# Moving the last softmax, four ternary weight slices, the first FFN product and the last FFN outputs of a transformer block on one core

## The reference

```
x = x + xattn(layernorm(x), ctx_768)        # keys and values from 1601 context rows
x = x + attn(layernorm(x))                  # 16 heads, softmax over 64 keys
x = x + ffn(layernorm(x))

scores = einsum('bhid,bhjd->bhij', q, k) / sqrt(dh)
scores = clip(scores, -1e5, 1e5) + einsum('bhid,ijd->bhij', q, rel_pos)
attn = softmax(scores); attn = attn / (attn.sum(-1) + 1e-8)

scale = max(mean(|w|), 1e-8); w_t = clip(round(w / scale), -1, 1)   # ternary
out = gelu(x @ w_t1.T + b1) @ w_t2.T + b2                           # 2048 hidden units
```

## Time and profile before

| what | value |
|---|---|
| median of 3 runs | 558.68 us (558.35 to 562.51) |
| the profiled execution, own time | 557.74 us |
| its span | 556.0 us |
| busy share of the span: PE, DVE, ACT, POOL | 93%, 63%, 35%, 35% |
| mean granted PE clock | 0.991 of full |

### The profile page before, as it was taken

How to read it: one execution, slowest core, us unless ns; L and a number is a source line. 1 busy time by engine, 2 the same in 40 slices (tenths; PEclk the granted TensorE clock), 3 DMA queues, 4 the chain that set the end, 5 groups by cost and what they waited for, 6 DMA issues and landing times.

```text
span 556.0 us, 10383 instructions
## 1 busy us (share of the span) xinstructions
PE 517.0 (93%) x4137; PEld 295.8 (53%) x4137; DVE 349.0 (63%) x777; ACT 196.4 (35%) x455; POOL 193.7 (35%) x132
## 2 busy tenths in 40 slices
PE   4987789987999999999999999999988879999997
PEld 2634245653764855666485575666574334444443
DVE  5747484384768459377665845957596895435333
ACT  0333014424623541653373355145143552211110
POOL 0221234224306244440821524359364992000000
PEclk9997899999999999999999999999999999999999
DMA  8999599499499779859959986953527420002002
GB/s 294 418 381 418 194 361 374 148 367 302 178 386 254 282 285 269 325 208 367 264 208 382 256 309 242 230 195 146 115 77 190 152 75 1 0 1 77 0 2 75
DMA packets 42096, 122.45 MB, mean 220 GB/s; under 512 B 19640, under 2 KB 21432, under 8 KB 37312
## 3 DMA queue, kind: packets, MB, share of 16 engines
q1 hardware_dynamic: 24256, 109.20, 54.3%
q10 hardware_dynamic: 17792, 12.58, 9.6%
HBM read 111.29 MB, written 10.49 MB: 219 GB/s over the span
## 4 chain that ended last, share of the span: by engine, by line
PE 58%; DVE 14%; DMA 8%; issue 7%; POOL 5%; ACT 4%; SPq 3%; ACTq 0%; DVEq 0%; POOLq 0%
PE u_ps L927 12%; PE s_ps L1158 9%; PE w_ps L1143 8%; DMA area<-in_nat_dram 6%; PE u_ps L848 5%; PE s_ps L837 5%; PE w_ps L950 4%; DVE area L1253 3%; POOL area L418 2%; PE w_ps L859 2%; PE w_ps L941 2%; DMA area<-in_kt_dram 2%; PE w_ps L913 1%; DVE area L1343 1%; DVE area L1301 1%
## 5 line engine op out<-in xcount | busy, mean ns | idle before, releaser
L1253 DVE BATCH_NORM_STATS2 area<-area 128x6 f32<-128x384 f32 (+1 forms) x208 | 99.8, 546 | 30.1 <-DMA area<-in_nat_dram 30.1
L927 PE MATMUL u_ps<-area 128*64 128x384 f32 (+1 forms) x416 | 74.1, 500 | 5.0 <-DVE area L1319 5.0
L837 PE MATMUL s_ps<-area 128*64 128x512 f32 (+1 forms) x384 | 69.2, 503 | 2.4 <-DMA area<-in_kt_dram 1.3
L1158 PE MATMUL s_ps<-area 128*128 128x512 f16 x256 | 60.2, 378 | 4.8 <-DVE area L1557 4.8
L453 POOL TENSOR_SCALAR area<-area 128x512 f16<-128x512 f32 x32 | 55.8, 1760 | 15.3 <-DMA area<-in_wf_dram 15.3
L1143 PE MATMUL w_ps<-area 128*128 128x512 f16 x256 | 60.7, 378 | 0.2 <-ACT area L734 0.2
L418 POOL TENSOR_TENSOR area<-area 128x16 f32<-128x16 f32 (+1 forms) x16 | 39.1, 2441 | 48.0 <-DVE area L1268 48.0
L734 ACT ACTIVATE area<-w_ps,area 128x512 f32<-128x512 f32 x32 | 22.0, 688 | 79.4 <-PE w_ps L1143 74.0
L927 PEld LDWEIGHTS u_ps<-area 128*64 128x64 f32 (+1 forms) x416 | 27.9, 137 | 39.2 <-issue 30.8
L1301 DVE CUSTOM_DVE_ANT_0 area<-w_ps,area 128x512 f32<-128x512 f32 x24 | 15.4, 690 | 52.6 <-PE w_ps L810 52.6
L837 PEld LDWEIGHTS s_ps<-area 128*64 128x64 f32 x384 | 23.2, 136 | 40.0 <-issue 35.4
(11 more groups left out here) (177 smaller groups left out, 832.4 us busy)
## 6 DMA issues: line engine op xcount, KB each, us to landing
area<-in_kt_dram SPq DMA_DIRECT2D x24, 1536.0 KB, 8.4
area<-in_nat_dram SPq DMA_DIRECT2D x48, 768.0 KB, 9.6
area<-in_wf_dram SPq DMA_DIRECT2D x32, 256.0 KB, 8.8
skew<-area ACTq DMA_DIRECT2D x8, 1024.0 KB, 8.8
area<-in_wf_dram SPq DMA_DIRECT2D x16, 512.0 KB, 3.4
area<-in_aw_dram SPq DMA_DIRECT2D x4, 1024.0 KB, 12.9
area<-skew ACTq DMA_DIRECT2D x16, 256.0 KB, 12.9
area<-in_x_dram SPq DMA_DIRECT2D x8, 256.0 KB, 11.3
```

Of the source, the lines that this page charges most:

```text
L837: ins = pe.matmul(S[ch][u * L:(u + 1) * L, 0:n], a_sb[:, c, u * L:(u + 1) * L], x[:, u, c, :], start=(c == 0), stop=(c == KC - 1))
L927: ins = pe.matmul(U[u * L:(u + 1) * L, 0:DC], pT[g % 2][0:m, i, u * L:(u + 1) * L], nat[0:m, j, u, :], start=(j == 0), stop=(j == NJ - 1))
L1158: ins = pe.matmul(S[q], g[i % 3][:, q * P:(q + 1) * P], wf16[:, f, 1, :], start=(f == 0 and z == 0), stop=(f == KF - 1 and z == 1))
L1253: dve.bn_stats(st[b][0:m, 2 * j + u, :], nat[0:m, j, u, :]).then_inc(s["key_stats"], 1)
```

## The change

1. **Last softmax.** The operations of tile 7 stand apart, one behind the `parts` of a slice each: add at i = 1, maximum at 2, subtraction at 3, exponential on ACT at 5, `row_scale` behind `parts(5)`, product behind `parts(6)`. `PROBS_AT` goes from 6 to 8, `VALUES_AT` from 8 to 10, `O_AT` from 9 to 11, `Z7_AT` from 12 to 14, `Z6_AT` from 1 to 2.
2. **Ternary slices.** Slices 0 to 2 lie over the folded query-key weights, slice 3 over another row that is free by then, so `ternary(0)` to `ternary(3)` stand in step 7. Eleven slices stand before the loop instead of eight. POOL's comparisons move with them: `neg(5)` into step 7, `neg(6)` to `neg(10)` ahead of the reciprocal root of tile 6.
3. **First FFN product.** `hidden(0)` stands ahead of `att_o(6)` and `values(7)` on PE.
4. **Last outputs.** `last_out` does the two last output steps token tile by token tile: for each of the four tiles the matmuls of i = 30 and i = 31, then its semaphore.
5. In step 7 ACT does `cT_out` and `skew_load` ahead of `ctx_out`; in the bridge the softmax of tile 6 starts ahead of `v_out(6)`.

```diff
-        wf16, at = carve(NAT_AT, [P, KF, 2, CW], F16)
+        wf16, at = [], WQK_AT
+        for f in range(KF):
+            if f == 3:
+                assert at <= WQK_END
+                at = WROW_AT
+            elif f == 4:
+                at = NAT_AT
+            v, at = carve(at, [P, 2, CW], F16)
+            wf16.append(v)
-        AHEAD = HIGH_ON_ACT = 8
-        Z6_AT, PROBS_AT, VALUES_AT, O_AT, Z7_AT, EXP_AFTER = 1, 6, 8, 9, 12, 2
+        AHEAD, HIGH_ON_ACT = 11, 8
+        Z6_AT, EXP_AT, PROBS_AT, VALUES_AT, O_AT, Z7_AT = 2, 5, 8, 10, 11, 14
...
@@ gpsimd
                     neg(4)
+                    neg(5)
...
             row_rstd(LAST_T - 2, "ln2_var", "ln2_rstd", VE2, RS2)
-            neg(5)
+            neg(6)
             add_fb2(LAST_T - 2)
-            for f in range(6, 8):
+            for f in range(7, 11):
                 neg(f)
             row_rstd(LAST_T - 1, "ln2_var", "ln2_rstd", VE2, RS2)
             add_fb2(LAST_T - 1)
-            for f in range(8, KF):
+            for f in range(11, KF):
                 neg(f)
@@ scalar, step
                     probs_out(r)
+                if not more:
+                    cT_out(p)
+                    skew_load(t)
+                if r is not None:
                     ctx_out(r)
-                cT_out(p)
-                if t is not None:
+                if more:
+                    cT_out(p)
+                if t is not None and more:
                     skew_load(t)
@@ tensor
+            def last_out():
+
+                h = 1
+                for q in range(4):
+                    for i in (2 * KF - 2, 2 * KF - 1):
+                        if q == 0:
+                            pe.wait_ge(s["gelu_low"], i + 1)
+                        for z, g in enumerate((gh, gl)):
+                            ins = pe.matmul(S[q], g[i % 3][:, q * P:(q + 1) * P], wf16[i - h * KF][:, 1, :], start=False,
+                                            stop=(i == 2 * KF - 1 and z == 1))
+                    ins.then_inc(s["ffn_out_ps"], 1)
+
+            hidden(0)
+            att_o(LAST_T - 1)
+            values(LAST_T)
+            for i in range(1, 2 * KF):
...
-                if i < 2 * KF:
-                    hidden(i)
+                hidden(i)
                 if i >= 2:
                     ffn_out(i - 2)
+            last_out()
@@ vector, ternary
                 if f == 0:
+                    dve.wait_ge(s["a_ps"], NT)
+                if f == 3:
+                    dve.wait_ge(s["cq_terms"], NT)
+                if f == 4:
                     dve.wait_ge(s["tile_weighted"], NJ * NT)
@@ vector, step
                 pt_scale(p, 2)
+                if not more:
+                    ternary(0)
                 pt_scale(p, 3)
                 if not more:
+                    ternary(1)
+                    ternary(2)
                     return
@@ vector, bridge
-            v_out(LAST_T - 1)
-            row_shift(LAST_T - 1)
-            ternary(3)
+            row_add(LAST_T - 1)
+            row_max(LAST_T - 1)
+            row_shift(LAST_T - 1)
+            v_out(LAST_T - 1)
             row_scale(LAST_T - 1)
+            row_product(LAST_T - 1)
             z_low(LAST_T - 2)
-            ternary(4)
+            ternary(6)
             clip(LAST_T)
-            ternary(5)
+            ternary(7)
+            ternary(8)
             x2_sum(LAST_T - 1)
             x2_norm(LAST_T - 1)
-            ternary(6)
+            ternary(9)
             v_out(LAST_T)
-            ternary(7)
+            ternary(10)
@@ vector, loop
-                if i == EXP_AFTER:
-                    row_shift(LAST_T)
-                if i == EXP_AFTER + 1:
-                    row_scale(LAST_T)
-                if i == O_AT:
-                    x2_sum(LAST_T)
+                if i == O_AT + 1:
                     x2_norm(LAST_T)
                 parts(i)
+                if i == EXP_AT - 4:
+                    row_add(LAST_T)
+                if i == EXP_AT - 3:
+                    row_max(LAST_T)
+                if i == EXP_AT - 2:
+                    row_shift(LAST_T)
+                if i == EXP_AT:
+                    row_scale(LAST_T)
+                if i == EXP_AT + 1:
+                    row_product(LAST_T)
+                if i == O_AT:
+                    x2_sum(LAST_T)
                 if i + AHEAD < KF:
                     ternary(i + AHEAD)
```

More of the change, by code:

```diff
@@ L87, in build_program @@
         small, at = carve(at, [P, 160])
+        WQK_AT = at
         wqk, at = carve(at, [P, KD, DC + 2])
+        WQK_END = at
         xwvo, at = carve(at, [P, KC, D])
@@ L113, in build_program @@
         zn = yn
+        WROW_AT = at
         wrow, at = carve(at, [P, D])
@@ L1124, in _ @@
             att_values(LAST_T - 1)
-            att_o(LAST_T - 1)
-            values(LAST_T)
             def hidden(i):
@@ L1142, in hidden @@
                     for z in range(2):
-                        ins = pe.matmul(HID[i % 2][:, :], wf16[:, f, 0, c * P:(c + 1) * P], zt[:, 4 * h:4 * h + 4, z, c, :], start=(k == 0),
+                        ins = pe.matmul(HID[i % 2][:, :], wf16[f][:, 0, c * P:(c + 1) * P], zt[:, 4 * h:4 * h + 4, z, c, :], start=(k == 0),
                                         stop=(k == 2 * KD - 1))
@@ L1157, in ffn_out @@
                     for z, g in enumerate((gh, gl)):
-                        ins = pe.matmul(S[q], g[i % 3][:, q * P:(q + 1) * P], wf16[:, f, 1, :], start=(f == 0 and z == 0),
+                        ins = pe.matmul(S[q], g[i % 3][:, q * P:(q + 1) * P], wf16[f][:, 1, :], start=(f == 0 and z == 0),
                                         stop=(f == KF - 1 and z == 1))
@@ L1163, in ffn_out @@
                     ins.then_inc(s["ffn_step"], 1)
-            for i in range(2 * KF + 2):
+            def last_out():
[12 more added lines that the diff above has]
+            for i in range(1, 2 * KF):
                 if i == Z6_AT:
@@ L1334, in clip, with row_add, row_max, row_shift @@
                                   1e5, -1e5, ALU.min, ALU.max).then_inc(s["clip_done"], 1)
-            def row_shift(t):
-                if t >= LAST_T - 1:
-                    dve.wait_ge(s["clip_done"], t + 1)
-                    dve.wait_ge(s["skew_loaded"], 32 * (t + 1))
-                    dve.tensor_tensor(ssb, ssb, rsk, ALU.add).then_inc(s["radd_done"], 1)
+            def row_add(t):
+                dve.wait_ge(s["clip_done"], t + 1)
+                dve.wait_ge(s["skew_loaded"], 32 * (t + 1))
+                dve.tensor_tensor(ssb, ssb, rsk, ALU.add).then_inc(s["radd_done"], 1)
+            def row_max(t):
                 dve.wait_ge(s["radd_done"], t + 1)
                 dve.tensor_reduce(rows16[:, 0, :], ssb, AX.X, ALU.max).then_inc(s["rowmax_done"], 1)
+            def row_shift(t):
                 dve.wait_ge(s["rowmax_done"], t + 1)
@@ L1360, in row_scale, with row_product @@
                 dve.tensor_tensor(rows16[:, 4, :], rows16[:, 4, :], rows16[:, 2, :], ALU.mult).then_inc(s["row_scale_step"], 1)
[L1361 to L1363 removed]
+            def row_product(t):
+                dve.wait_ge(s["row_scale_step"], 5 * (t + 1))
+                dve.tensor_tensor(psb, psb, rows16[:, 4, :].unsqueeze(2).to_broadcast([P, H, L]), ALU.mult).then_inc(s["probs_ready"], 1)
             def v_out(t):
@@ L1427, in ternary @@
                 if f == 0:
+                    dve.wait_ge(s["a_ps"], NT)
+                if f == 3:
+                    dve.wait_ge(s["cq_terms"], NT)
+                if f == 4:
                     dve.wait_ge(s["tile_weighted"], NJ * NT)
                 for w in range(2):
-                    dve.scalar_tensor_tensor(out=wf16[:, f, w, :], in0=wraw[f % 4][:, w, :], scalar=sm(WTHR + w), in1=wneg[f % 4][:, w, :],
+                    dve.scalar_tensor_tensor(out=wf16[f][:, w, :], in0=wraw[f % 4][:, w, :], scalar=sm(WTHR + w), in1=wneg[f % 4][:, w, :],
                                              op0=ALU.is_gt, op1=ALU.subtract).then_inc(s["ternary_done"], 1)
@@ L1479, in step @@
                 if r is not None:
+                    row_max(r)
                     row_shift(r)
@@ L1522, in _ @@
                 step(n)
-            ternary(0)
+            ternary(3)
             clip(LAST_T - 1)
-            ternary(1)
+            ternary(4)
             x1_sum(LAST_T)
@@ L1528, in _ @@
             x2_sum(LAST_T - 2)
-            ternary(2)
+            ternary(5)
             x2_norm(LAST_T - 2)
+            row_add(LAST_T - 1)
+            row_max(LAST_T - 1)
+            row_shift(LAST_T - 1)
             v_out(LAST_T - 1)
-            row_shift(LAST_T - 1)
-            ternary(3)
             row_scale(LAST_T - 1)
+            row_product(LAST_T - 1)
             z_low(LAST_T - 2)
-            ternary(4)
+            ternary(6)
             clip(LAST_T)
-            ternary(5)
+            ternary(7)
+            ternary(8)
             x2_sum(LAST_T - 1)
             x2_norm(LAST_T - 1)
-            ternary(6)
```

(3 more changed lines are left out.)

5 lines of the change are left out of this document (1 added, 4 removed).

## The result

The changed kernel takes 556.44 us (median of 8, 555.66 to 557.98) against 560.10 us for the kernel before (median of 8, 558.35 to 562.51). The ratio is 0.9933, 95% interval 0.9909 to 0.9957: 3.7 us shorter, more than the uncertainty and less than the 1% called a plain difference ahead of the prediction. The forecast was 554.9 us from a median of 558.68, a step of -3.8 us.

The account below looks back on a forecast made before the run. DVE and POOL were taken to set the pace from 435 to 461 us, PE afterwards. Loop -3.0, bridge and step 7 -0.05, last outputs -0.74 sum to -3.8: from 558.68 to 554.9 us, range 551.5 to 557.9.

Parts of the forecast that it names:

- rival A: FFN loop: DVE's length decides when the softmax product is ready; the forecast itself, 554.9 us, chance 0.62.
- part 2: Spread softmax in the FFN loop: DVE's sum of 24.7 us behind v_out(7) ends att_turn(7) earlier, -3.0 us.
- the text's own sign of being wrong: Wrong if DVE's mean ternary operation between v_out(7) and the product is far from 0.98 us.
- Part 1: hidden(0) ahead of att_o(6): fills PE's 0.74 us wait, delays the chain behind by 1.0 us; z_turn(6) still waits about 1.
- Part 3: Ternary slices moved into step 7 and bridge cost nothing there; three of 1.76 us leave the stretch before the product.
- Part 4: Bridge: softmax of tile 6 without a ternary slice inside counts nothing; cT_out ahead of ctx_out in step 7, 0.05 us.
- Part 5: Kernel's end: last outputs token tile by token tile let DVE keep up with PE, -0.74 us.
- B: FFN loop: PE's own length decides, all waits but that for v_out(7) vanish; -7.0, 551.7 us, chance 0.18.
- D: Before the loop: tile 6's root on POOL is late behind slice 10's load; net +3.5, 562.2 us, chance 0.07.
- E: FFN loop: DVE and POOL exclude each other, their operations run in one line; net +5.4, 564.1 us, chance 0.03.

Follow-up runs that it names:

- e3: Changed kernel with hidden(0) back behind att_o(6) and values(7): median 556.44 us, ratio 0.9922; att_values(6) to last result 129.9 us.
- e5: Changed kernel with ternary slices and POOL's comparisons placed as before the change, softmax still spread: median 562.01 us, ratio 1.0013; att_values(6) to last result 135.2 us.
- e2: Changed kernel with the two last output steps one after the other, as before: median 557.38 us, ratio 0.9923; att_values(6) to last result 130.9 us.
- e4: Changed kernel without POOL's comparisons of slices 11 to 15 (a probe, other values): median 553.39 us, ratio 0.9871; att_values(6) to last result 127.2 us.
- e11: Changed kernel with tile 7's turns one slice later, add_fb2(6) behind the comparisons, ternary(9) before x2_sum(6): 552.81 us, ratio 0.9854; att_values(6) to last result 126.2 us.
- e6: Changed kernel with tile 7's turns one slice later (9, 11, 12, 15): median 555.72 us, ratio 0.9896; att_values(6) to last result 128.9 us.
- e12: e11 with hidden(0) also put back behind att_o(6) and values(7): median 553.98 us, ratio 0.9898; att_values(6) to last result 127.1 us.
- e13: Changed kernel run once more, unedited, as control: median 556.35 us, ratio 0.9937; att_values(6) to last result 130.4 us.
- e1: Changed kernel with tile 7's softmax back in two bursts and its turns as before: median 560.49 us, ratio 0.9998; att_values(6) to last result 134.4 us.
- e10: Changed kernel with POOL's add_fb2(6) behind the comparisons of slices 11 to 15: median 555.67 us, ratio 0.9888; att_values(6) to last result 130.2 us.

## Why the prediction was right

The step, -3.8 us, and the sign were right, and the mechanism it rested on (rival A) is what the profile shows: PE waits in front of `ffn_out` for `parts` and in front of `att_turn(7)` for the product. That the size of the loop's term came out so near is in part luck, as part 2 shows. By its own parts:

**Part 2, the loop, -3.0.** Measured by the mark, the end of `att_turn(7)` counted from the start of `att_values(6)`: 41.0 us before (460.32 - 419.29) and 37.7 after (458.79, where the next product begins, - 421.06): -3.3. The product ended 24.6 us behind `v_out(7)` against 24.7 forecast. Inside, errors cancelled, and the text's own sign of being wrong was not clear of it: it asked for a mean ternary operation near 0.98 us between `v_out(7)` and the product, and the twelve there had 0.849, 13% less. The six ternary slices took 9.3 us, not 10.6, because three of them were not disturbed (1.33 a pair); the spread softmax operations and `row_scale` were 0.6 us shorter together; `parts` were as summed, 5.3. Against that DVE waited 1.74 us for POOL, 1.38 of it for slice 11, where the sum had 0.5. The sum checked POOL at slice 15 alone; the rows before the change had 1.6 us of such waits, 1.38 of them at the second slice behind `v_out(7)`.

**Where PE waits.** I forecast four waits of 0.3 to 0.4 us ahead of `ffn_out(0)`, (2), (3) and (4) and about 2 us for the product. There were three, of 0.37, 0.52 and 0.34, ahead of (1), (2) and (4), and 1.21 us. The places are off by the short and long pairs above. The size is off because I filled PE's time with groups of 1.74 us. Every row of eight matmuls shows 1.90, of which the last 0.16 is overlapped by the next group, but only if there is no wait between them:

```profile
435.67 1.89 PE L1173 MATMUL s_ps<-area 128*128 128x512 f16 x8
437.40 1.90 PE L1158 MATMUL w_ps<-area 128*128 128x512 f16 x8
439.67 1.90 PE L1173 MATMUL s_ps<-area 128*128 128x512 f16 x8 [0.37 <-DVE area L1606]
```

The first two start 1.73 us apart. The third starts 2.27 us behind the second: 1.90 and the wait of 0.37. So each wait costs 0.16 us more than its idle time, four times over. Work and waits together are as forecast.

**Part 1, the first product.** `z_turn(6)` waited 0.80 us (forecast about 1), `att_o(6)` not at all. That the move is a cost and not a gain at this place is shown by e3, at 0.5 us; part 1's delay of 1.0 us was right as a length of the chain (counted from `att_values(6)`, `att_o(6)` started 0.96 us later and `v_out(7)` 0.84) and too large as an effect on the end.

**Part 3, the slices.** I costed their new places at nothing, which held: the way through step 7 and the bridge took no longer (72.09 against 72.20 us). But the text valued the shift at three slices of 1.76 us taken out ahead of the product, since DVE "had 7 to 15 to do". That is misread. In the kernel before, slices 7 to 10 stood between `v_out(7)` and the product; two of these four pairs are in the earlier trace rows, the others are

```profile
434.07 1.83 DVE L1430 SCALAR_TENSOR_TENSOR area<-area 128x512 f16<-128x512 f32 x2 [1.38 <-POOL area L453]
437.37 1.83 DVE L1430 SCALAR_TENSOR_TENSOR area<-area 128x512 f16<-128x512 f32 x2 [0.20 <-POOL area L453]
```

With the softmax spread there are six pairs (10 to 15), and seven (7 to 13) if the slices are not shifted, as in e5. So the shift takes one pair out of the way, and POOL's work beside the rest. The sum itself counts six and is not touched. e5 measured 3.2 us of waits and 1.6 of clock for it. The two parts are not additive: either one undone, with all other numbers kept, gives the whole gain back.

**Part 4, the bridge.** `att_turn(6)` waited 1.01 instead of 1.16 us, and PE still waited 0.53 us for ACT's copies, as before. Step 7 and the bridge together gave 0.1 us. Nothing, as counted. The two reorderings of item 5 of the change, on ACT in step 7 and in the bridge, were not undone one by one.

**Part 5, the end, -0.74.** The last result ended 0.70 us nearer the last matmul, and the first group of `last_out` cost 0.1 us: e2 gives 0.6 for the whole. The term was slightly too large. From the mark to the last result the time fell from 93.1 to 92.6 us; with the 3.3 us ahead of the mark that is the 3.8 us of the stretch.

**The rivals.** B's price, -7.0, is nearly that of e4 (134.1 to 127.2), and e11 goes below it without taking POOL's work away (126.2, -7.9): its mechanism was priced right and its condition is not met by the changed kernel. D's margin held: the load of slice 10 took 5.1 us, the comparison ran 3.10 us behind it, and POOL was free 0.6 us before the root was due, inside the 0.3 to 1.0 of the text. E, and with it the rule of the page "SBUF — State Buffer" in the Trainium skill, section "Who interferes with whom", read as full blocking, is not borne out here: with POOL busy the twelve ternary operations grew from 737 to 849 ns in the mean. Their lengths had a median of 740 and a longest of 1174 ns, so an operation lost up to 0.44 us beside comparisons of 1.56 to 2.52 us and never the length of one. That the two disturb each other it states rightly, and e4 puts 3.2 us on it.

**What stays open.** I did not try a version in which POOL's comparisons are kept out of DVE's way by their place rather than removed, so how much of e4's 3.2 us is disturbance and how much is waiting is known from the rows alone. The code before step 7, the same in all versions, starts the stretch between 419.3 and 423.0 us in different runs; the last section shows one place where some of that arises, the rest was not studied.

## What to carry to other kernels

When two engines in order feed the busy one, sum the feeding engine's work up to each point that is waited for, its disturbed length included, and place the waiting instruction where that sum ends; here moving a number by one slice (e6) was worth 1.4 us, and that with two changes of order (e11) 4.2. Filling a short wait of the bound engine pays only if nothing behind the filler starts the chain that sets the next wait (e3 against e12). To compare parts of a microsecond, take a stretch of the trace that all kernels share, and run one of them twice (e13).

## What the runs showed of the hardware

PE's granted clock fell behind long waits. Windows of e5, where PE had just waited 4.02 us for the product, and of e1, where it had just waited 3.90 us for `parts(2)` (length, PE busy, clock, DMA):

```profile
461.00:466.00 5.00, 5.00 (x21) 0.66 0.00 0
466.00:480.00 14.00, 14.00 (x118) 1.00 0.00 1
```

```profile
447.00:452.00 5.00, 4.91 (x15) 0.66 0.00 0
452.00:480.00 28.00, 27.24 (x182) 1.00 0.00 1
```

A mean of 0.66 over 5 us is 3.4 us at the lower of the two levels (1.2 GHz) and the rest at the higher (2.4 GHz). It doubled the length of the matmuls in that time and cost about 1.6 us in e5. With waits of 2.1 and 2.7 us before the change, and 2.21 in e10, the clock stayed at 1.00 in the loop. So a single wait near 4 us cost more than its own length here, which is one more reason for spreading work in front of several short waits. That the wait is the cause was seen twice and not tried by itself.

The length of the last wait alone does not tell when. At 135 us, in code that is the same in all versions, PE does four short matmuls between two waits and then twelve longer ones. In the changed kernel's two traces, first run and e13:

```profile
135.37 2.80 PE L854 MATMUL s_ps<-area 128*64 128x512 f32 x12 [2.23 <-DMA area<-in_kt_dram]
```

```profile
132.09 0.66 PE L1030 MATMUL w_ps<-area 128*128 128x128 f32 x4 [1.37 <-DVE area L1435]
134.80 4.49 PE L854 MATMUL s_ps<-area 128*64 128x512 f32 x12 [2.05 <-DMA area<-in_kt_dram]
```

Behind the wait of 2.23 us the clock stayed at 1.00. Behind that of 2.05 us, with one of 1.37 just before it, the twelve took 1.7 us longer, and the mean clock from 130 to 140 us was 0.83. Eight of the twelve traces show 0.83 there and four, the kernel before among them, 1.00. This is one source of the different starts of the stretch.
